# A Mamba block with a mixture of experts on one core: y's gating moves from the recurrence to GpSimd in the third stage

## Chip, cores and metric

One core of one Trainium2 chip (trn2). The metric is the device time of one execution in microseconds (us), the median of several runs. Engines are named as in the profile: PE (TensorE), DVE (VectorE), ACT (ScalarE), POOL (GpSimd), SP (SyncE, which here only issues DMAs).

## The reference

For 2048 tokens of width 512 (`x`), with `xn = layernorm(x)`, the kernel computes `x + mamba(xn) + moe(xn)`:

```python
proj = xn @ in_proj_w.T                       # 2048 x 2048
x, gate = split(proj, 2)                      # 1024 channels each
xc = silu(causal_conv(x, conv_w, 4 taps) + conv_b)
ts, B, C = split(xc @ x_proj_w.T, [32, 48])   # 16 states
dt = softplus(ts @ dt_proj_w.T + dt_proj_b)
state = state * exp(dt * A) + dt * B * xc     # one after the other over the 2048 tokens
y = sum_over_states(state * C) + xc * D
y = y * silu(gate)
mamba = y @ out_proj_w.T
```

`moe` picks 6 of 64 experts for each token (capacity 64; each expert is a SwiGLU from 512 to 352 and back) and adds a shared SwiGLU of width 704.

## The kernel before

The program has three stages. The first (`stage1`) does the layernorm, the routing, the input projection, the convolution and the gates. It stores in HBM, for each of 32 tiles, the convolved x (`xt_d`) and silu of the gate (`sz_d`), each 128 channels by 512 tokens.

The second stage, the recurrence, has 32 steps. A step i is one of 4 chunks c of 512 tokens and one of 8 blocks d of 128 channels; at the same time it does one pair of the 64 experts. Inside a step, 8 groups g of two states each run through the engines:

- PE makes dt*B*x in PSUM (`p_dBx`, L1334), with two buffers, so group g+2 starts when DVE has scanned group g.
- ACT makes exp(dt*A) (`dA`, L1173), with four buffers, so it runs four groups ahead of DVE.
- DVE scans the two states (L1023) from `dA` and `p_dBx`.
- POOL multiplies the scanned states by C (L959).
- PE sums them over the states into `p_y` (L1343), four groups at a time.

Between its groups PE does the experts' three matmuls (gate and up L1303, down L1320) and dt of the next step. Next to its scans DVE does three things. After g=1 it finishes dt of the next step (L990) and multiplies it by x (`dt_x`, L997). After g=4 it multiplies the y of the step before by silu of the gate (`gate`, L1005). After g=5 and g=6 it does the experts' products (L1040, L1044). ACT, at the end of a step, puts x*D into `p_y` (`x_times_D`, L1129), which has to wait until DVE has read the old `p_y`; PE's sum of the first four groups adds to it (`start=False`) and so waits for ACT.

What goes in which order is written out by hand: each engine runs its own list in order, and semaphores tie them. All of SP's transfers go through one queue. In step i SP issues, in this order: the next dt weights (L1462), the next gate weights of 1408 KB (L1454), C of the next chunk (L1516), 16 transfers of 64 KB that spread dt over the partitions (`spread_dt`, L851), the silu tile (L877), the store of y (L878), the up weights of 1408 KB (L1458), x of step i+2 (`load_xa`, L1450, after the sum of the first four groups, because until then `x_times_D` reads the buffer), and the down weights of 1408 KB in three transfers with rows of 2 KB (L844).

The third stage goes over the 4 chunks. For each, PE does 5.5 tiles of the shared SwiGLU (L1392) and then 14 tiles of the output sum (`out_tiles`, L1403): k = 0 to 7 are the 8 blocks of gated y, loaded as `gc` into the state's buffer; k = 8 to 13 are the shared part. Each operand is split in two parts for the matmul: ACT writes the high part (L1236, and L1216 for the shared weights), DVE subtracts it from the source to get the low part (`k_lo` L1058, `w_lo` L1052, `x_lo` L1063, `DVE out_operand_parts`, `shared_w_parts` and `x_parts` in the trace). Both parts have two buffers. POOL adds up the residuals of the chunk (L973, L977). SP loads `gc`, then the residual's inputs, then stores the four output tiles.

## Time and profile before

| | us |
|---|---|
| median of 3 runs | 1344.96 (1337.76 to 1350.12) |
| profiled execution | 1337.05 |
| its span in the trace | 1335.2 |
| busy: PE, DVE, ACT, POOL | 1233.3, 1078.3, 894.6, 866.8 |
| first stage and start of the second, about | 0 to 266 |
| recurrence, about | 266 to 1041 |
| third stage, about | 1041 to 1335 |

The span is what lies between the first and the last recorded instruction; the execution's time is 1.85 us longer. Times below are us from the start of the span. A group of instructions is named by its line, its engine and its tile; "idle before" is the time in which the engine stood still just before such an instruction, and what ended it.

### The profile page before, as it was taken

Reading aid. Unit: us, or ns where it says so; the run is one execution under the profiler, and the core shown is the slowest. Engines: PE = TensorE matmul, PEld = TensorE weight load, DVE = VectorE, ACT = ScalarE, POOL = GpSimd, SP = SyncE. Lnnn points to the kernel's source line nnn. Section 1 sums busy time; section 2 is a strip of 40 time slices with the busy share of each in tenths; the row PEclk is TensorE's granted clock in tenths of the full one; section 3 lists DMA queues with packets and bytes.
Section 4 is the critical chain, followed back from the end, with each engine's and each line's share of the span. In section 5 each row is a group of like instructions: output and inputs, shape, how many; then the busy total and the mean of one; then the engine's idle time right before and its main releaser. Section 6 shows DMA issues by size and latency. Waiting matters only on the chain.

```text
span 1335.2 us, 53004 instructions
## 1 busy us (share of the span) xinstructions
PE 1233.3 (92%) x21558; PEld 796.7 (60%) x21558; DVE 1078.3 (81%) x1235; ACT 894.6 (67%) x1925; POOL 866.8 (65%) x456
## 2 busy tenths in 40 slices
PE   6999999399999999999899998999999999999998
PEld 4777767255555555555555554455555678787876
DVE  5989888489999979899899987899999564646554
ACT  4766667287897977978878897678777243424343
POOL 3445467188989979899889997889989340303030
PEclk9999999699999989999999998999999999999999
DMA  8364554779999989999999999899898843122130
GB/s 269 122 261 160 180 207 143 244 213 283 296 302 281 319 251 274 298 282 321 281 258 316 275 309 283 260 280 290 255 325 260 282 182 139 51 102 87 63 125 31
DMA packets 131714, 305.90 MB, mean 229 GB/s; under 512 B 18400, under 2 KB 22752, under 8 KB 129824
## 3 DMA queue, kind: packets, MB, share of 16 engines
q1 hardware_dynamic: 124048, 286.18, 65.8%
q0 software_dynamic: 7600, 18.91, 7.1%
q8 instruction: 33, 0.54, 0.2%
q14 instruction: 33, 0.27, 0.1%
HBM read 214.04 MB, written 57.69 MB: 204 GB/s over the span
## 4 chain that ended last, share of the span: by engine, by line
PE 37%; ACT 11%; DMA 8%; DVE 8%; issue 8%; SPq 6%; ACTq 1%; POOL 1%; DVEq 0%; POOLq 0%
PE p_dBx L1392 7%; PE p_dBx L1334 7%; DVE state L1023 5%; SPq L851 5%; ACT dA L1173 4%; DMA xt_for_dtx<-xt_d 4%; PE p_y L1343 3%; PE p_g L1320 3%; DMA dt_blocks_odd<-step_rows 3%; PE p_y L1403 3%; PE p_g L1403 2%; PE p_u L1403 2%; PE p_dt L1403 2%; PE p_u L1303 2%; PE p_g L1303 2%
## 5 line engine op out<-in xcount | busy, mean ns | idle before, releaser
L1023 DVE TENSOR_TENSOR_SCAN state<-dA,state_carry,p_dBx 128x512 f32<-128x512 f32 x512 | 617.7, 1261 | 44.4 <-PE p_dBx L1334 42.2
L959 POOL TENSOR_TENSOR h_times_C<-state,C_bcast 128x1024 f32<-128x1024 f32 x128 | 305.0, 2388 | 62.5 <-DVE state L1023 60.9
L959 POOL TENSOR_TENSOR C_bcast<-state,C_bcast 128x1024 f32<-128x1024 f32 x128 | 315.9, 2611 | 20.4 <-DVE state L1023 19.3
L1334 PE MATMUL p_dBx<-B_diagonals,step_rows 64*32 64x128 f32 x16384 | 295.3, 275 | 29.2 <-DVE state L1023 20.1
L1334 PEld LDWEIGHTS p_dBx<-B_diagonals,step_rows 64*32 64x32 f32 x16384 | 233.2, 106 | 142.3 <-issue 140.6
L1173 ACT ACTIVATE dA<-dt_blocks_odd,A_par 128x512 f32<-128x512 f32 x256 | 169.4, 709 | 40.5 <-DMA dt_blocks_odd<-step_rows 40.5
L1173 ACT ACTIVATE dA<-dt_blocks_even,A_par 128x512 f32<-128x512 f32 x256 | 169.4, 709 | 29.5 <-DMA dt_blocks_even<-step_rows 29.5
L288 POOL TENSOR_TENSOR w_in_parts_lo<-C_bcast,w_in_parts_hi 128x512 fp32r<-128x512 f32 x64 | 96.2, 1504 | 95.2 <-ACT w_in_parts_hi L505 94.9
L973 POOL TENSOR_TENSOR step_rows<-step_rows 128x512 f32<-128x512 f32 x16 | 22.0, 1407 | 181.8 <-DMA step_rows<-moe 181.8
L384 DVE SCALAR_TENSOR_TENSOR conv_out<-conv_in,conv_w,conv_out 128x512 f32<-128x512 f32 x96 | 107.4, 1127 | 16.2 <-ACT conv_out L529 13.9
L1303 PE MATMUL p_g<-w_gate_pair,step_rows 128*64 128x352 f32 x512 | 85.0, 473 | 9.4 <-ACT step_rows L1184 9.1
L1320 PE MATMUL p_g<-w_down_pair,step_rows 128*64 128x512 f32 (+1 forms) x396 | 92.3, 601 | 0.0
L505 ACT ACTIVATE w_in_parts_hi<-C_bcast 128x512 fp32r<-128x512 f32 x64 | 40.3, 631 | 70.5 <-PE p_in L664 62.0
L1303 PE MATMUL p_u<-w_up_pair,step_rows 128*64 128x352 f32 x512 | 85.4, 475 | 2.1 <-issue 2.1
L664 PE MATMUL p_in<-xT_parts_hi,w_in_parts_lo 128*128 128x512 f32 x256 | 73.3, 408 | 8.1 <-POOL w_in_parts_lo L288 6.8
L1222 ACT ACTIVATE shared_h_rows<-p_dBx 128x512 f32<-128x512 f32 (+1 forms) x24 | 14.4, 598 | 98.2 <-PE p_dBx L1392 97.7
L1392 PE MATMUL p_dBx<-x_parts,shared_w_parts_even 128*128 128x512 f32 x288 | 69.7, 399 | 2.4 <-DVE shared_w_parts_even L1052 2.4
L1343 PE MATMUL p_y<-h_times_C,sum_over_states 128*32 128x512 f32 x512 | 62.1, 598 | 7.7 <-ACT p_y L1129 6.7
L664 PE MATMUL p_in<-xT_parts_lo,w_in_parts_hi 128*128 128x512 f32 x256 | 69.2, 392 | 0.0
L664 PE MATMUL p_in<-xT_parts_hi,w_in_parts_hi 128*128 128x512 f32 x256 | 68.5, 389 | 0.0
L945 POOL DMA_INDIRECT moe<-expert_y,scatter_lists x33 | 54.2, 1641 | 20.0 <-ACT expert_y L1145 15.0
L1074 DVE TENSOR_TENSOR shared_h_rows<-shared_h_rows,p_dBx 128x512 f32<-128x512 f32 (+1 forms) x24 | 16.5, 686 | 61.7 <-ACT shared_h_rows L1222 61.5
(185 smaller groups left out, 2062.3 us busy)
## 6 DMA issues: line engine op xcount, KB each, us to landing
w_gate_pair<-in_w_gate SPq DMA_DIRECT2D x32, 1408.0 KB
w_up_pair<-in_w_up SPq DMA_DIRECT2D x32, 1408.0 KB
w_down_pair<-in_w_down SPq DMA_DIRECT2D x66, 512.0 KB
dt_blocks_odd<-step_rows SPq DMA_DIRECT2D x256, 64.0 KB
dt_blocks_even<-step_rows SPq DMA_DIRECT2D x240, 64.0 KB
w_down_pair<-in_w_down SPq DMA_DIRECT2D x33, 384.0 KB
g_d<-y_gated SPq DMA_DIRECT2D x33, 256.0 KB, 3.8
sz_d<-silu_gate SPq DMA_DIRECT2D x32, 256.0 KB, 2.2
```

Source lines behind the costliest of these rows:

```text
L288: pool.tensor_tensor(wp[1][:, n % 2, :], win[:, tile, :], wp[0][:, n % 2, :], ALU.subtract).then_inc(s_wlo, 1)
L384: ins = dve.scalar_tensor_tensor(xt[:, d, :], xr[:, d, k:k + CH], cw[:, d, k:k + 1], xt[:, d, :], ALU.mult, ALU.add)
L664: ins = pe.matmul(pIn[n % 2][:, :], wp[p][:, n % 2, k * P:(k + 1) * P], xp[q][:, c % 2, k, :], start=at == 0, stop=at == len(parts) - 1)
L959: pool.tensor_tensor(hc[m][:, b, :, :], hb[:, q, :, :], Cb[:, NM * (c % 2) + GS * m:NM * (c % 2) + GS * m + GS, :], ALU.mult).then_inc(s_h ...
L1023: ins = dve.tensor_tensor_scan(hb[:, g % NBUF, s, :], dA[:, g % NBUF, s, :], pB[:, g % 2, :].rearrange("p (t s) -> p s t", s=GS)[:, s, :], ...
L1173: ins = act.activation(dA[:, q, s, :], dtr[u][:, b, :], ACT.Exp, scale=A[:, bass.ds(d, 1), GS * g + s:GS * g + s + 1].rearrange("p a b -> ...
L1303: ins = pe.matmul(pX[r, 0:I], xgT[:, k, r], w[:, a, k, :], start=k == 0, stop=k == KH - 1)
L1320: ins = pe.matmul(pG[r, :], hT[0:k, m, r], wd[0:k, a, m, :], start=m == 0, stop=m == len(IK) - 1)
L1334: ins = pe.matmul(out[DB * p:DB * p + DB, half, j, :, :], dtxT[k, j * P + DB * b:j * P + DB * b + DB], diag[k, ND * cp + 2 * j + p // 2, a ...
L1343: ins = pe.matmul(pY[DB * b:DB * b + DB, :], sel4[:, :], hc[m][:, b, s, :], start=False, stop=m == 1 and s == GS - 1, skip_group_check=True)
L1392: ins = pe.matmul(pX[m % 2][:, :], wparts[m % 2][:, 2 * w + a, k, :], xp[x][:, k, :], start=at == 0, stop=at == len(parts) - 1)
L1403: ins = pe.matmul(pO[j][:, :], k_parts(p, k, 0)[:, j * P:(j + 1) * P], k_parts(q, k, 1), start=k == 0 and at == 0, stop=k == NK - 1 and at ...
```

## The change

The recurrence stores y without D*x and without the gate: ACT copies `p_y` to SBUF (`take_y`, after its `dA` of g=6), PE starts the sum fresh, and DVE's `gate` and ACT's `x_times_D` are gone. In the third stage POOL gates the 8 tiles of a chunk, three instructions each (x times D, plus y, times silu), from two buffers of x and silu that SP loads tile by tile (`gate_inputs`). ACT's `k_hi` waits for the gated tile. The buffer of `gc` is loaded for the next chunk as soon as DVE has made the low parts of its 8 tiles. The down weights lie in HBM and SBUF so that both experts of a pair are one run of 4 KB. x of step i+2 is loaded ahead of the spread of dt.

```diff
-            def x_times_D(i, u, d):
-                act.wait_ge(s_xa, 16 * i + 16)
-                act.wait_ge(s_g, i + 1)
-                act.activation(pY[:, :], xa[:, u, :], ACT.Copy, scale=d).then_inc(s_xD, 1)
+            def take_y(n, u):
+                act.wait_ge(s_gst, 16 * n + 16)
+                act.wait_ge(s_sum, 2 * n + 2)
+                act.activation(gb[:, u, :], pY[:, :], ACT.Copy).then_inc(s_y, 1)
...
-            def gate(n, u):
-                dve.wait_ge(s_gst, 16 * n + 16)
-                dve.wait_ge(s_sz, 16 * n + 16)
-                dve.wait_ge(s_sum, 2 * n + 2)
-                dve.tensor_tensor(gb[:, u, :], pY[:, :], sz, ALU.mult).then_inc(s_g, 1)
...
             def load_wd(i):
                 for m, (at, k) in enumerate(IK):
-                    sp.dma_start(wd[0:k, :, m, :], io["w_down"][i][:, at:at + k, :].rearrange("a p h -> p a h")).then_inc(s_wd, 16)
+                    sp.dma_start(wd[0:k, m, :, :], io["w_down"][i][at:at + k, :, :]).then_inc(s_wd, 16)
+            def gate_inputs(c, d):
+                if ND * c + d >= 2:
+                    sp.wait_ge(s_g, ND * c + d - 1)
+                sp.dma_start(xa[:, d % 2, :], io["xt_d"][ND * c + d]).then_inc(s_gin[d % 2], 16)
+                sp.dma_start(sz[:, d % 2, :], io["sz_d"][ND * c + d]).then_inc(s_gin[d % 2], 16)
...
+                if i + 2 < STEPS:
+                    sp.wait_ge(s_dtx, i + 1)
+                    tile_in.load_xa(sp, i + 2)
                 if i + 1 < STEPS:
                     sp.wait_ge(s_dA, NG * i + 1)
                     spread_dt(i + 1)
-                sp.wait_ge(s_g, i + 1)
-                sp.dma_start(sz[:, :], io["sz_d"][i]).then_inc(s_sz, 16)
+                sp.wait_ge(s_y, i + 1)
                 sp.dma_start(io["g_d"][i], gb[:, 1 - i % 2, :]).then_inc(s_gst, 16)
...
-                sp.wait_ge(s_sum, 2 * i + 3)
-                if i + 2 < STEPS:
-                    tile_in.load_xa(sp, i + 2)
...
             sp.dma_start(gc, g_v[0]).then_inc(s_gc, 16)
+            for d in range(2):
+                gate_inputs(0, d)
...
             for c in range(1, NCH):
                 load_xT(sp, c)
+            for d in range(2, ND):
+                gate_inputs(0, d)
...
             residual_inputs(0)
-            store_out(0)
             for c in range(1, NCH):
-                sp.wait_ge(s_kused, NK * c + 2)
+                sp.wait_ge(s_klo, 2 * NK * (c - 1) + 2 * ND)
                 sp.dma_start(gc, g_v[c]).then_inc(s_gc, 16)
+                for d in range(2):
+                    gate_inputs(c, d)
+                store_out(c - 1)
+                for d in range(2, ND):
+                    gate_inputs(c, d)
                 residual_inputs(c)
-                store_out(c)
+            store_out(NCH - 1)
...
+            def gating(c, d):
+                if isinstance(d, int) and d == 0:
+                    pool.wait_ge(s_gc, 16 * c + 16)
+                pool.wait_ge(s_gin[d % 2], 16 * ND * c + 32 * (d // 2 + 1))
+                pool.tensor_tensor(xa[:, d % 2, :], xa[:, d % 2, :], Dp[:, d:d + 1].to_broadcast([P, CH]), ALU.mult).then_inc(s_xD, 1)
+                pool.wait_ge(s_xD, ND * c + (d + 1))
+                pool.tensor_tensor(gc[:, d, :], gc[:, d, :], xa[:, d % 2, :], ALU.add).then_inc(s_yD, 1)
+                pool.wait_ge(s_yD, ND * c + (d + 1))
+                pool.tensor_tensor(gc[:, d, :], gc[:, d, :], sz[:, d % 2, :], ALU.mult).then_inc(s_g, 1)
...
             scatter(STEPS)
+            for d in range(3):
+                gating(0, d)
             scatter(STEPS + 1)
+            for d in range(3, ND):
+                gating(0, d)
+            with pool.Fori(0, 1) as c:
+                residuals(c)
+            with pool.Fori(1, NCH) as c:
+                for d in range(ND):
+                    gating(c, d)
+                residuals(c)
...
             def k_hi(c, k):
                 act.wait_ge(s_kused, NK * c + (k + 1))
-                if k == 0:
-                    act.wait_ge(s_gc, 16 * c + 16)
+                if k < ND:
+                    act.wait_ge(s_g, ND * c + (k + 1))
...
                         ins = pe.matmul(pY[DB * b:DB * b + DB, :], sel4[:, :], hc[m][:, b, s, :],
-                                        start=False, stop=m == 1 and s == GS - 1, skip_group_check=True)
+                                        start=m == 0 and s == 0, stop=m == 1 and s == GS - 1, skip_group_check=True)
...
-                    pe.wait_ge(s_xD, i + 1)
+                    pe.wait_ge(s_y, i + 1)
                     sum_states(i, 0, 0)
```

SP's queue in one step of the recurrence before: `xt_for_dtx` is x of step i+2, `dt_blocks` the spread of dt.

```order
L1454 DMA w_gate_pair<-in_w_gate 128x2x1408 [waits expert_g_in_psum]
L1516 DMA C_bcast<-bc_d 32x512 [waits hc_ready]
L851 DMA dt_blocks_even<-step_rows 32x512 [waits dt_copied,dA_ready]
L851 DMA dt_blocks_even<-step_rows 32x512 x15
L877 DMA step_rows<-sz_d 128x512 [waits gated_ready]
L878 DMA g_d<-y_gated 128x512
L1458 DMA w_up_pair<-in_w_up 128x2x1408 [waits expert_u_in_psum]
L1450 DMA xt_for_dtx<-xt_d 128x512 [waits hc_summed]
L844 DMA w_down_pair<-in_w_down 128x2x512 [waits expert_y_in_psum]
```

The same stretch of SP's queue in the changed kernel:

```order
L1485 DMA w_gate_pair<-in_w_gate 128x2x1408 [waits expert_g_in_psum]
L1547 DMA C_bcast<-bc_d 32x512 [waits hc_ready]
L1481 DMA xt_for_dtx<-xt_d 128x512 [waits dtx_ready]
L852 DMA dt_blocks_odd<-step_rows 32x512 [waits dt_copied,dA_ready]
L852 DMA dt_blocks_odd<-step_rows 32x512 x15
L890 DMA g_d<-y_gated 128x512 [waits y_taken]
L1489 DMA w_up_pair<-in_w_up 128x2x1408 [waits expert_u_in_psum]
L845 DMA w_down_pair<-in_w_down 128x1024 [waits expert_y_in_psum]
```

x has moved from behind the up weights to just ahead of the spread of dt, and the silu tile is gone from the step.

SP's queue in the third stage before, from the load of one chunk's y to its stores:

```order
L927 DMA state<-g_d 128x8x512 [waits out_parts_used]
L914 DMA C_bcast<-in_x 128x4x512 [waits x_lo_ready,out_ready,residual_ready]
L915 DMA step_rows<-moe 128x4x512
L916 DMA step_rows<-moe 128x4x512
L921 DMA out<-y_gated 128x512 [waits out_ready] x4
```

The changed kernel, from the load of one chunk's y over the stores of the chunk before to the residual's inputs (two of the six later pairs of gate inputs are shown):

```order
L938 DMA state<-g_d 128x8x512 [waits out_lo_ready]
L858 DMA xt_for_dtx<-xt_d 128x512 [waits gated_ready]
L859 DMA gate_tiles<-sz_d 128x512
L858 DMA xt_for_dtx<-xt_d 128x512 [waits gated_ready]
L859 DMA gate_tiles<-sz_d 128x512
L933 DMA out<-y_gated 128x512 [waits out_ready] x4
L858 DMA xt_for_dtx<-xt_d 128x512 [waits gated_ready]
L859 DMA gate_tiles<-sz_d 128x512
L858 DMA xt_for_dtx<-xt_d 128x512 [waits gated_ready]
L859 DMA gate_tiles<-sz_d 128x512
```

Two tiles' inputs now stand ahead of the stores of the chunk before, six behind them, and the residual's inputs behind all of these.

POOL in the third stage of the changed kernel, the last tile of a chunk and what follows it:

```order
L987 TENSOR_TENSOR xt_for_dtx<-xt_for_dtx,D_par 128x512 [waits gate_inputs_loaded1]
L988 REGISTER_ALU
L989 TENSOR_TENSOR state<-state,xt_for_dtx 128x512 [waits x_times_D_ready]
L991 TENSOR_TENSOR state<-state,gate_tiles 128x512 [waits y_plus_xD_ready]
L995 ISA
L996 ISA [waits residuals_loaded]
L998 TENSOR_TENSOR step_rows<-step_rows 128x512 [waits shared_gu_in_psum]
```

In the kernel before, the first POOL instruction of a chunk is the residual's first addition; now 24 instructions stand ahead of it.

## Rows read from the trace of the kernel before

**Rows 1.** Busy time by window: PE, PEld, DVE, ACT, POOL; clock; DMA share; GB/s
```profile
266.00:1041.00 775.00, 720.94 (x19132) 397.31 (x19131) 705.05 (x677) 626.48 (x1471) 687.51 (x319) 0.99 0.94 282
1041.00:1120.50 79.50, 76.85 (x332) 58.34 (x332) 44.56 (x57) 31.14 (x53) 19.61 (x11) 0.98 0.50 179
1120.50:1190.50 70.00, 69.49 (x302) 55.97 (x301) 38.67 (x54) 27.25 (x47) 11.31 (x8) 1.00 0.26 90
900.20:922.55 22.35, 22.20 (x607) 12.33 (x602) 21.94 (x22) 18.16 (x41) 21.51 (x11) 1.00 0.91 265
```

**Rows 2.** DVE's waits, 266 to 1041: us in total, times, longest
```profile
DVE state L1023 <- PE p_dBx L1334: 42.2, 51, 3.7
DVE dt_x L997 <- DMA xt_for_dtx<-xt_d: 18.6, 16, 1.7
DVE p_dt L990 <- ACT step_rows L1115: 8.2, 11, 1.3
```

**Rows 3.** ACT's waits in the same stretch
```profile
ACT dA L1173 <- DMA dt_blocks_odd<-step_rows: 40.5, 14, 7.5
ACT dA L1173 <- DMA dt_blocks_even<-step_rows: 29.5, 12, 5.4
...
ACT p_y L1129 <- DVE y_gated L1005: 16.0, 15, 3.4
```

**Rows 4.** Groups of instructions, 266 to 1041: busy us, mean ns, idle before
```profile
L1005 DVE TENSOR_TENSOR y_gated<-p_y,step_rows 128x512 f32<-128x512 f32 x32 | 21.3, 667 | 0.0
...
L1129 ACT ACTIVATE p_y<-xt_for_dtx,D_par 128x512 f32<-128x512 f32 x32 | 21.8, 682 | 16.0 <-DVE y_gated L1005 16.0
```

**Rows 5.** Timeline of one step: start, duration, engine; x's issue and its use
```profile
697.85 0.52 SPq L1450 DMA_DIRECT2D xt_for_dtx<-xt_d  x1
...
706.35 0.69 DVE L997 TENSOR_TENSOR dt_x<-p_dt,xt_for_dtx 128x512 f32<-128x512 f32 x1 [1.43 <-DMA xt_for_dtx<-xt_d]
```

**Rows 6.** SP's timeline in another step: the spread of dt
```profile
883.26 10.12 SPq L851 DMA_DIRECT2D dt_blocks_even<-step_rows  x16
```

**Rows 7.** DVE's timeline in the third stage, before and while POOL adds residuals
```profile
1138.56 0.69 DVE L1052 TENSOR_TENSOR shared_w_parts_even<-w_gate_pair,shared_w_parts_even 128x512 fp32r<-128x512 f32 x1
...
1143.57 0.69 DVE L1074 TENSOR_TENSOR shared_h_rows<-shared_h_rows,p_dBx 128x512 f32<-128x512 f32 x1 [3.72 <-ACT shared_h_rows L1222]
...
1147.01 1.79 DVE L1058 TENSOR_TENSOR out_operand_parts<-state,out_operand_parts 128x512 fp32r<-128x512 f32 x1
```

**Rows 8.** POOL's timeline in the third stage: residual additions, chunk 0 (first half) and 1
```profile
1085.79 6.72 POOL L973 TENSOR_TENSOR step_rows<-step_rows 128x512 f32<-128x512 f32 x4 [23.38 <-DMA step_rows<-moe]
...
1140.33 5.04 POOL L973 TENSOR_TENSOR step_rows<-step_rows 128x512 f32<-128x512 f32 x4 [41.02 <-DMA step_rows<-moe]
1145.33 6.32 POOL L977 TENSOR_TENSOR C_bcast<-C_bcast,step_rows 128x512 f32 x4
```

**Rows 9.** PE's timeline, chunk 0: first matmuls of output tiles k = 2, 3, 6, 7
```profile
1084.70 0.84 PE L1403 MATMUL p_y<-out_operand_parts 128*128 128x512 f32 x3
...
1088.11 0.93 PE L1403 MATMUL p_y<-out_operand_parts 128*128 128x512 f32 x3 [0.52 <-DVE out_operand_parts L1058]
...
1098.30 0.93 PE L1403 MATMUL p_y<-out_operand_parts 128*128 128x512 f32 x3 [0.43 <-DVE out_operand_parts L1058]
...
1101.11 0.84 PE L1403 MATMUL p_y<-out_operand_parts 128*128 128x512 f32 x3
```

**Rows 10.** SP's timeline at the start of the third stage
```profile
1043.84 0.37 SPq L895 DMA_DIRECT2D state<-g_d  x1
...
1059.87 2.81 SPq L900 DMA_DIRECT2D w_down_pair<-in_sw_down  x6
```

**Rows 11.** DMA issues: count, KB each, median us from issue to landing
```profile
state<-g_d SPq DMA_DIRECT2D x4, 2048.0 KB, 8.6
step_rows<-moe SPq DMA_DIRECT2D x8, 1024.0 KB, 14.1
...
h_times_C<-in_w_out SPq DMA_DIRECT2D x1, 2048.0 KB, 10.5
```

47 lines of the change are left out of this document (24 added, 23 removed).

## The prediction

> **What bounds the kernel now.** I read the busy table by window first, then the waits of the engine that is busiest in the long window, then the timelines where the change puts work. The window from 266 to 1041 is the recurrence: in its 775 us DVE is busy 705.05 and PE 720.94 [rows 1]. The reader is to see that two engines are nearly full at once. DVE's waits there are 42.2 us on PE's `p_dBx`, 18.6 on the load of x and 8.2 on ACT's part of dt [rows 2]; with 705.05 that makes 774, so DVE's list accounts for the whole stretch, 24.2 us a step over 32 steps. One step, from 900.20 to 922.55, shows the pace when nothing is late: 22.35 us, with PE busy for 22.20 of it [rows 1]. PE's own work is therefore about 22.35 a step, and 32 x 22.35 = 715 us is the least that the recurrence can take while its matmuls stay as they are. At most 60 us can be won there.
>
> In the third stage the picture is another one. From 1120.5 to 1190.5, one chunk, PE is busy 69.49 of 70.00 us, DVE 38.67, ACT 27.25 and POOL 11.31 [rows 1]. PE bounds it without gaps, so nothing can be won there, and what is added to POOL costs time only where it makes PE wait.
>
> **The change part by part: the recurrence.** DVE loses 32 gates of 667 ns, 21.3 us; ACT swaps one copy of 682 ns for another of the same shape, at no cost, and loses the 16.0 us for which the old one waited for the gate [rows 3, 4]. The gate stands after the scan of g=4, just where PE has the up matmuls between its groups; in the step of 22.35 us the gate was in DVE's list and PE still hardly idled [rows 1]. There the 667 ns are hidden and their removal gives nothing: DVE will wait for `p_dBx` instead. In steps where DVE is late for another reason they count. The bounds are 0 and 21.3; I take a third, 7 us, because the unhurried step is the nearest row.
>
> The wait for x, 18.6 us in 16 steps [rows 2], goes: x was issued at 697.85, behind 1408 KB of up weights, and DVE used it at 706.35 after a wait of 1.43 [rows 5]. It now has a whole step. What is late next is the spread of dt. Its 16 issues take SP 10.12 us [rows 6], and ACT already waits 40.5 + 29.5 = 70 us for its blocks [rows 3]. x's 256 KB now stand directly ahead of it; at the 282 GB/s of the stretch [rows 1] that is 0.9 us more, against the same amount saved by the silu tile that no longer comes. ACT runs four groups ahead of DVE, so most of its lateness never reaches DVE; what did is the 8.2 us. I count 14 of the 18.6 us, and 3 of the 8.2 because dt is made earlier. The bounds are 6 (the spread takes over most of the wait) and 27 (all of both).
>
> Together the recurrence wins 7 + 14 + 3 = 24 us, between 6 and 46; the upper end leaves 729 us, or 22.8 a step, as close to PE's pace as I allow, since a new chunk and the first steps also cost.
>
> The down weights in runs of 4 KB: I cost this at 0. No row has one transfer in both forms; the nearest are two loads of 2048 KB, y in 2 KB runs in 8.6 us and the output weights in 16 KB runs in 10.5 with other loads ahead [rows 11], which show no gain of long runs. The bounds are -5 and +2. The Trainium skill, "DMA: Bandwidth & Descriptors", section "Specifications", asks for 512 B or more for line rate, which both forms have; by it the term is 0, too, and no run here shows 4 KB.
>
> **The change part by part: the third stage.** POOL gets 32 tiles of three dependent instructions, 96 in all. Alone, a sum of two 128x512 tiles takes POOL 5.04 / 4 = 1.26 us, beside a busy DVE 6.32 / 4 = 1.58 to 6.72 / 4 = 1.68 [rows 8]. With about 0.15 us for each wait between them (an estimate) a tile is 4.2 us alone and 5.2 when DVE is busy. The Trainium skill, "GPSIMD Engine Reference", section 3.1, gives about 2.6 cycles for an element of a two-input operation at 1.2 GHz; as an estimate from that page 512 elements are 1.11 us and a tile 3.8, which would end chunk 0's gating 3 us sooner and make this term 33 instead of the 36 below.
>
> The price is on DVE. While POOL adds, a DVE subtraction with both inputs in SBUF takes 1.79 us instead of 0.69; the product with an input in PSUM stays at 0.69 [rows 7]. An output tile then costs PE (1098.30 - 1088.11) / 3 = 3.40 us instead of 2.72 to 2.81 [rows 9], so each 3.4 us of POOL work beside the output tiles cost 0.68.
>
> Chunk 0: y's load is issued at 1043.84 [rows 10], and with the weights ahead of it the first tile can start at about 1060. Tiles 0 and 1 follow, but the inputs of tile 2 stand behind the shared down weights and three loads of xn, 4.5 MB in all, issued from 1059.87 on [rows 10], so they land at about 1076. Tiles 2 to 7 and the scatter between them then take 6 x 4.9 + 1.6 = 31 us, to 1107. Tile k = 7 started at 1101.11 [rows 9] and now starts at about 1107.5: +6. The residual's inputs are issued only when tile 5 is gated (about 1097) and take 14.1 us [rows 11], so POOL's additions, 13.5 us, lie beside k = 8 to 12, where DVE also does `x_lo` of the next chunk: two tiles with 3 contended subtractions (5.3 us instead of 2.7) and two with 2, 2 x 2.6 + 2 x 0.7 = 6.6. Chunk 0 costs +13.
>
> Chunks 1 to 3: tiles 0 and 1 are gated beside the last output tiles of the chunk before (9 us of POOL, +1.7, for chunks 1 and 2 booked there). Tiles 2 to 7 start about 6 us after the chunk, behind four stores, and end at about +34. From +23 (the product at 1143.57 in a chunk that began at 1120.5 [rows 7]) to +38 DVE has 12 subtractions for the last shared and the first output operands; contended, they take 12 x 1.79 = 21 us instead of 8, and k = 1 and 2 wait about 2. The residual's inputs are issued at about +24, when tile 5 is gated, and land at about +36 with nothing ahead of them, so its additions now lie beside output tiles k = 2 to 6 and cost another 4. That is 8 for each of chunks 1 and 2, and 7 for chunk 3 without a following one.
>
> The third stage loses 13 + 8 + 8 + 7 = 36 us. The bounds are 10 (POOL's phases fall between DVE's; chunk 0 alone pays) and 60 (every one of the 96 instructions delays one DVE subtraction by 1.1 us, 106 us, of which the idle half of DVE hides less than half).
>
> **The sum.** -24 + 36 = +12. Against the profiled execution, 1337.05, that is 1349; the median of the runs shown is 7.9 higher, which would make it 1357. I say 1353, between the two. Of a difference of 1%, 13 us, a measurement of this kernel can about tell that it is one; my sum lies just at that edge.
>
> **The rivals.**
> 1. The recurrence falls to PE's pace: with neither gate nor late x, DVE is ahead of PE in nearly every step, and the mean step goes from 24.2 to 22.8 us, -46, while the third stage costs half of my sum, 20. For it speaks the step of 22.35 us; against it, that 42.2 us of DVE's waits are on PE already. It decides if the mean step is under 23.0 us. Time: 1345 - 26 = 1319, faster.
> 2. The spread of dt takes x's place: its wait on ACT grows, dt comes late, and the recurrence wins only 6; the third stage costs 36. For it speak the 70 us of ACT's waits and the place of x in the queue. Time: 1345 + 30 = 1375, slower.
> 3. POOL's work is mostly hidden: the contended subtractions fall into DVE's idle half, the third stage costs only what chunk 0's late tiles and the residual's new place cost, 20, and the recurrence wins 24. Time: 1345 - 4 = 1341, no change.
>
> **How the numbers follow.** My forecast has 0.40, of which 0.29 is slower by over 1% and 0.11 within. Rival 1 has 0.20 (faster 0.19, same 0.01). Rival 2 has 0.16, all slower. Rival 3 has 0.24: faster 0.04, same 0.19, slower 0.01. So faster 0.23, same 0.31, slower 0.46. The range from 1320 to 1381 reaches from rival 1 to somewhat past rival 2; the likeliest case's own range is 1340 to 1366.
>
> **What would show it.** Right: no wait of `dt_x` on `xt_for_dtx`; DVE's waits on `p_dBx` larger than 42.2 us; a mean step near 23.4; in the third stage `out_operand_parts` and `shared_w_parts` on DVE often at 1.3 to 1.8 us; ACT waiting for POOL's gated tile at k = 3 to 7 of chunk 0; residual additions beside the output tiles; chunks of 77 to 78 us instead of 70. Wrong: chunks still of 70 to 72 us, or a recurrence under 735 us.

## The result, and the profile after

The changed kernel takes 1370.1 us (median of 4 runs, 1361.2 to 1379.9), the kernel before in runs beside it 1347.5 (1337.8 to 1355.8): the ratio is 1.0185 with a 95% interval of 1.0139 to 1.0231, slower by some 23 us. The profiled executions stand at 1365.71 (span 1363.9) and 1337.05 (span 1335.2); that of before is the fastest of its runs, so differences against it come out some 6 us too large, and the place for that is the recurrence: in every profile taken of a kernel with the old third stage, that stage took 292 to 294 us.

Busy time of the changed kernel by window (the recurrence, then the four chunks of the third stage), with the columns of [rows 1]:

```profile
266.00:1031.00 765.00, 744.27 (x19118) 404.45 (x19120) 680.34 (x641) 624.16 (x1470) 683.93 (x318) 1.00 0.93 275
1038.80:1133.50 94.70, 82.67 (x332) 61.12 (x332) 59.45 (x55) 28.88 (x50) 59.73 (x40) 0.93 0.62 215
1133.50:1209.00 75.50, 70.77 (x302) 55.59 (x301) 52.72 (x54) 27.36 (x47) 47.08 (x32) 1.00 0.42 139
1209.00:1285.10 76.10, 71.11 (x301) 55.51 (x301) 56.00 (x54) 27.35 (x47) 47.74 (x32) 1.00 0.40 138
1285.10:1359.20 74.10, 70.62 (x301) 55.67 (x300) 49.28 (x50) 25.54 (x46) 38.70 (x26) 1.00 0.29 101
```

The same windows of the third stage in the kernel before, as far as [rows 1] lacks them:

```profile
1041.80:1120.50 78.70, 76.85 (x332) 58.34 (x332) 43.76 (x56) 30.34 (x52) 18.95 (x11) 0.98 0.50 179
1190.50:1260.30 69.80, 69.48 (x301) 55.97 (x300) 38.50 (x54) 27.25 (x47) 11.33 (x8) 1.00 0.25 90
1260.30:1330.50 70.20, 69.59 (x301) 55.99 (x300) 36.36 (x50) 25.57 (x46) 11.79 (x8) 1.00 0.26 91
```

The chunks are 16.0, 5.5, 6.3 and 3.9 us longer: the third stage loses 31.7. The recurrence, which should have given 24 back, gave 3: its first step begins 0.4 us later than before, and the third stage starts at 1038.8 instead of 1041.8. (From the first to the last step it is 6 us shorter, 745.0 instead of 750.8; PE then stands 4.7 us for the first shared weights instead of 2.4.) Where the gain went is read from the waits (us in total, times, longest) from 266 to 1041. The changed kernel's:

```profile
DVE state L1055 <- PE p_dBx L1365: 81.9, 116, 4.8
...
PE p_g L1334 <- ACT step_rows L1213: 2.9, 5, 1.1
PE p_dBx L1365 <- DVE state L1055: 1.6, 4, 0.5
```

PE's in the kernel before:

```profile
PE p_dBx L1334 <- DVE state L1023: 20.1, 16, 2.2
PE p_g L1303 <- ACT step_rows L1184: 9.1, 10, 1.2
...
PE p_y L1343 <- ACT p_y L1129: 6.7, 15, 0.6
PE p_dt L1283 <- ACT step_rows L1137: 4.6, 3, 3.2
```

DVE's waits for x, 18.6 us [rows 2], are gone, and so are the gates, 21.3 us [rows 4]; nearly all of it, 39.7 us, reappears as waiting for PE, 81.9 instead of 42.2. PE's own waits fell from 20.1 + 9.1 + 6.7 + 4.6 = 40.5 us to 4.5. So PE should have been done 36 us sooner. It was not, because its own matmuls took longer. The two groups that grew (busy us, mean ns of one, idle before), before:

```profile
L1334 PE MATMUL p_dBx<-B_diagonals,step_rows 64*32 64x128 f32 x16320 | 293.3, 275 | 28.6 <-DVE state L1023 20.1 <-issue 8.4
L1343 PE MATMUL p_y<-C_bcast,sum_over_states 128*32 128x512 f32 x512 | 62.0, 598 | 0.0
```

and after:

```profile
L1365 PE MATMUL p_dBx<-B_diagonals,step_rows 64*32 64x128 f32 x16320 | 303.5, 274 | 15.9 <-issue 13.4 <-DVE state L1055 1.6
L1374 PE MATMUL p_y<-C_bcast,sum_over_states 128*32 128x512 f32 x512 | 84.8, 600 | 0.8
```

The same 512 sums over the second half of the states fill 84.8 us instead of 62.0, the same dBx matmuls 303.5 instead of 293.3: 33 us more, with an unchanged duration of the single matmul. Sixteen sums of 0.6 us each take 1.92 us, so they run side by side; the time grows when they start one behind the other. The start flag that the change adds is not it: it stands on the other half of the sums, which took 62.1 in both. That was the question for the experiments: what makes PE slower as soon as it no longer waits?

### The profile page after: what moved, and what is told of

Same layout as the page of the kernel before. It is cut to its first block, busy times and chain, and to the rows that moved or that the text cites. A ratio compares the mean times of both kernels' runs of the same rounds, so it can differ in the third digit from the quotient of the medians.

```text
span 1363.9 us, 53050 instructions
## 1 busy us (share of the span) xinstructions
PE 1268.5 (93%) x21558; PEld 805.1 (59%) x21558; DVE 1120.4 (82%) x1202; ACT 893.4 (66%) x1926; POOL 1009.8 (74%) x551
## 4 chain that ended last, share of the span: by engine, by line
PE 59%; DVE 7%; issue 5%; ACT 3%; DMA 3%; POOL 3%; SPq 1%; ACTq 0%; DVEq 0%; POOLq 0%
PE p_dBx L1365 18%; PE p_y L1374 9%; PE p_dBx L1423 6%; PE p_g L1351 6%; PE p_g L1334 5%; PE p_u L1334 5%; DVE out_operand_parts L1088 4%; PE p_y L1434 2%; PE p_u L1434 1%; PE p_g L1434 1%; PE p_dt L1434 1%; PE p_u L1320 1%; DVE state L1055 1%; DMA dt_blocks_odd<-step_rows 1%; PE p_dt L1327 1%
## 5 line engine op out<-in xcount | busy, mean ns | idle before, releaser
L1055 DVE TENSOR_TENSOR_SCAN state<-dA,state_carry,p_dBx 128x512 f32<-128x512 f32 x512 | 619.7, 1262 | 82.0 <-PE p_dBx L1365 81.9
L975 POOL TENSOR_TENSOR C_bcast<-state,C_bcast 128x1024 f32<-128x1024 f32 x128 | 319.7, 2731 | 8.3 <-DVE state L1055 7.9
L1365 PE MATMUL p_dBx<-B_diagonals,step_rows 64*32 64x128 f32 x16384 | 305.5, 274 | 16.6 <-issue 13.4
L1365 PEld LDWEIGHTS p_dBx<-B_diagonals,step_rows 64*32 64x32 f32 x16384 | 236.4, 105 | 137.0 <-issue 134.1
L987 POOL TENSOR_TENSOR xt_for_dtx<-xt_for_dtx,D_par 128x512 f32<-128x512 f32 x32 | 42.1, 1316 | 79.8 <-DMA gate_tiles<-sz_d 79.7
L1374 PE MATMUL p_y<-C_bcast,sum_over_states 128*32 128x512 f32 x528 | 86.7, 600 | 0.8
L1434 PE MATMUL p_y<-out_operand_parts 128*128 128x512 f32 (+1 forms) x168 | 51.5, 415 | 25.2 <-DVE out_operand_parts L1088 24.9
L664 PE MATMUL p_in<-xT_parts_lo,w_in_parts_hi 128*128 128x512 f32 x256 | 68.9, 391 | 0.0
L1423 PEld LDWEIGHTS p_dBx<-x_parts,shared_w_parts_even 128*128 128x128 f32 x288 | 54.7, 192 | 19.1 <-issue 7.4
```

The source lines that it names most:

```text
L664: ins = pe.matmul(pIn[n % 2][:, :], wp[p][:, n % 2, k * P:(k + 1) * P], xp[q][:, c % 2, k, :], start=at == 0, stop=at == len(parts) - 1)
L975: pool.tensor_tensor(hc[m][:, b, :, :], hb[:, q, :, :], Cb[:, NM * (c % 2) + GS * m:NM * (c % 2) + GS * m + GS, :], ALU.mult).then_inc(s_h ...
L1055: ins = dve.tensor_tensor_scan(hb[:, g % NBUF, s, :], dA[:, g % NBUF, s, :], pB[:, g % 2, :].rearrange("p (t s) -> p s t", s=GS)[:, s, :], ...
L1365: ins = pe.matmul(out[DB * p:DB * p + DB, half, j, :, :], dtxT[k, j * P + DB * b:j * P + DB * b + DB], diag[k, ND * cp + 2 * j + p // 2, a ...
L1374: ins = pe.matmul(pY[DB * b:DB * b + DB, :], sel4[:, :], hc[m][:, b, s, :], start=m == 0 and s == 0, stop=m == 1 and s == GS - 1, skip_gro ...
L1423: ins = pe.matmul(pX[m % 2][:, :], wparts[m % 2][:, 2 * w + a, k, :], xp[x][:, k, :], start=at == 0, stop=at == len(parts) - 1)
```

## The experiments

In the tables below the recurrence is measured in each profile from the first to the last step's down matmuls, the third stage from the first shared tile to the end; the ratio is to the kernel before, run beside each.

```
kernel                     recurrence  third stage  median us  ratio [95%]
before                        750.8       293.4       (1348-1352)
changed                       745.0       325.1       1370.1   1.0185 [1.0139, 1.0231]
e1  sum moved                 749.0       328.6       1375.2   1.0188 [1.0153, 1.0223]
e2  dt projection twice       768.2       324.8       1386.4   1.0272 [1.0241, 1.0303]
e3  no gating                 752.4       312.9       1359.1   1.0066 [1.0041, 1.0091]
e4  x early alone             770.3       292.3       1352.3   1.0025 [0.9993, 1.0057]
e5  indirect DMAs moved       720.4       323.6       1344.0   0.9971 [0.9944, 0.9998]
e6  before, DMAs moved        784.1       293.2       1373.2   1.0159 [1.0113, 1.0204]
e7  x early, DMAs moved       770.4       293.8       1362.3   1.0097 [1.0065, 1.0129]
e8  tiles 2, 3 first          746.7       321.6       1366.8   1.0141 [1.0100, 1.0183]
e9  one product               735.3       301.8       1333.5   0.9864 [0.9826, 0.9901]
e10 no indirect DMAs          701.5       324.6       1319.3   0.9763 [0.9731, 0.9795]
e11 residuals first           751.8       294.5       1344.1   0.9950 [0.9920, 0.9980]
e12 4 KB weights alone        763.1       292.3       1344.9   0.9987 [0.9961, 1.0013]
```

### e1 and e2: is PE short of instructions?

```diff
-                    dBx(i, cp, 2)
                     sum_states(i, 1, 1)
+                    dBx(i, cp, 2)
```

> The changed kernel, with PE's sum over the second half of the states (16 matmuls) moved from behind the third dBx group of a step to ahead of it, right behind the gate matmuls. In the changed kernel this sum takes 2.5 to 3.0 us in 25 of 32 steps where it took 1.92 before, and a step takes 23.8 us though PE waits for nothing. Theory A (a TensorE that never waits is short of instructions: it uses up its lead in the dBx groups, 128 instructions in 1.09 us each, and the sum behind them then gets its instructions late and loses the step between its four column groups): behind the slow gate matmuls the lead is there, the sum takes 1.92 us again, a step 22.6 to 23.0 us, and the recurrence is 25 to 35 us shorter than in the changed kernel: some 1338 us. Theory B (the sum is slow because of what it reads or of the flag that starts its accumulation, wherever it stands): it stays at 2.5 to 3.0 us, a step at 23.8 us and the time within 5 us of the changed kernel's.

Measured: all 33 sums at 1.92 us, and yet nothing gained. PE waits for DVE's scans again, which it had stopped doing; the third dBx group now stands 1.9 us later, and DVE gets its input late. The row of PE's waits, 266 to 1041:

```profile
PE p_dBx L1365 <- DVE state L1055: 37.1, 31, 1.2
```

Both theories missed. What stays: in e1, as in the kernel before, PE waits over a microsecond a step (37.1 us in 31 waits) and has fast sums.

```diff
                 pe.wait_ge(s_wdt, 32 * n + 32)
+                pe.matmul(pM[:, :], wdt[:, :], ts[:, :], start=True, stop=True)
                 pe.matmul(pM[:, :], wdt[:, :], ts[:, :], start=True, stop=True).then_inc(s_dtps, 1)
```

> The changed kernel, with the dt projection of each step (one 512-column matmul of 0.49 us) made twice, to the same result: PE gets more work, in which few instructions pass. Theory A (short of instructions): the half microsecond lets the instructions catch up, the sum over the second half of the states falls from 3.0 to 1.92 us in most steps, and a step is not longer than 23.8 us, rather 23.1 to 23.4: the whole 10 to 20 us faster than the changed kernel although PE does more. Theory B (the sum is slow for another reason): the sum stays at 2.5 to 3.0 us, a step is 0.4 us longer, the whole 10 to 15 us slower than the changed kernel.

Measured: slower by another 16 us, and the sums at 1.92 us. Theory A had the sums right, but falls: time to catch up gives nothing back. Theory B had the time about right, but falls too, for the stall left the sum and went into the dBx group ahead of it. One step of e2 beside one of the changed kernel shows where it stays. First e2 (start, duration; PE and GpSimd's gather):

```profile
617.93 1.06 PE L1366 MATMUL p_dBx<-B_diagonals,step_rows 64*32 64x128 f32 x51
618.55 1.01 POOL L953 DMA_INDIRECT tokens_of_pair<-xn_d,gather_lists  x1
619.19 0.28 PE L1366 MATMUL p_dBx<-B_diagonals,step_rows 64*32 64x128 f32 x1 [0.19 <-issue]
619.93 0.50 PE L1366 MATMUL p_dBx<-B_diagonals,step_rows 64*32 64x128 f32 x12 [0.46 <-issue]
```

Then the changed kernel, with the weight load (PEld) at which the sum's stall ends, and its other stall, in the last dBx group beside the scatter:

```profile
622.90 1.60 POOL L961 DMA_INDIRECT moe<-expert_y,scatter_lists  x1 [0.15 <-issue]
623.30 0.84 PE L1365 MATMUL p_dBx<-B_diagonals,step_rows 64*32 64x128 f32 x35
624.30 0.72 PE L1365 MATMUL p_dBx<-B_diagonals,step_rows 64*32 64x128 f32 x29 [0.16 <-issue]
...
634.14 1.01 POOL L953 DMA_INDIRECT tokens_of_pair<-xn_d,gather_lists  x1
634.38 3.03 PE L1374 MATMUL p_y<-C_bcast,sum_over_states 128*32 128x512 f32 x16
...
635.50 0.17 PEld L1374 LDWEIGHTS p_y<-C_bcast,sum_over_states 128*32 128x32 f32 x7 [0.63 <-issue]
```

In e2 PE stalls behind its 51st dBx matmul, in the changed kernel within the sum: other instructions. But the stall ends 619.93 - 618.55 = 1.38 us after the gather's start in the one and 635.50 - 634.14 = 1.36 in the other. It is so in the whole recurrence: at 28 of the 31 gathers of the changed kernel from 286 us on, and at all 31 of e2, an idle time of 0.4 to 0.8 us of the weight loads, put down to "issue", ends 1.27 to 1.38 us after the gather's start. It keeps time with GpSimd, not with PE's program, and "issue" says that PE waited for nothing that the profile shows. The stall shown is over 1.36 us after the start, while the gathers of this kernel land 8.8 us after theirs (median). The Trainium skill, "Perfetto Trace Analysis", section "DMA Instruction — SWDGE (GPSIMD)", says that such a row lasts until the descriptors are written, not until the data are there. The trace agrees, with a row of 1.01 us; by that, the stall shown, from 634.87 to 635.50, lies in the time in which GpSimd's cores write descriptors (until 635.15) and just behind it.

The gather of the kernel before stands at the same place, and its sums don't suffer (start and duration):

```profile
343.85 1.01 POOL L937 DMA_INDIRECT tokens_of_pair<-xn_d,gather_lists  x1 [0.16 <-issue]
344.08 1.92 PE L1343 MATMUL p_y<-C_bcast,sum_over_states 128*32 128x512 f32 x16
```

That gave theory C: PE gets no new instructions while GpSimd starts an indirect DMA (the instruction that fetches or adds rows by a list of indices, here the gather and the scatter), and a PE that has waited in this step or the last has some in store.

### e5 and e10: move the indirect DMAs, leave them out

```diff
-GATHER_AT, SCATTER_AT = 0, 4
+GATHER_AT, SCATTER_AT = 0, 5
...
+                    if g == GATHER_AT:
+                        pool.wait_ge(s_xT, i + 1)
+                        gather(i + 1)
                     pool.wait_ge(s_sum, 2 * i + (m + 1))
...
-                    if g == GATHER_AT:
-                        pool.wait_ge(s_xT, i + 1)
-                        gather(i + 1)
```

> The changed kernel, with GpSimd's two indirect DMAs of a step moved: the gather ahead of the step's first product with C instead of behind it, so that it falls beside PE's gate matmuls (32 instructions in 2.5 us), the scatter one product later, beside the down matmuls. The extra dt projection did not bring the time of the sum back: PE's stalls only moved in its program, and stayed where they were against GpSimd: 0.7 us from 0.6 us after a gather's start, 0.6 us from 0.9 us after a scatter's. Theory C (while GpSimd starts an indirect DMA TensorE gets no new instructions, and loses what it has not in store; the kernel before had them in store because PE waited over a microsecond a step): the sum over the second half of the states takes 1.92 us in nearly all steps, the last dBx group 1.09 us instead of 1.77, a step 22.5 to 23.3 us instead of 23.8, the recurrence 15 to 35 us shorter than in the changed kernel: 1335 to 1355 us. Rival D (the stalls belong to PE's own program and only keep step with GpSimd): they stay in the sum and in the last dBx group, a step at 23.6 to 24 us and the time within 6 us of the changed kernel's.

Measured: 26 us faster than the changed kernel, the recurrence 24.6 shorter. The groups of e5, 266 to 1007:

```profile
L1365 PE MATMUL p_dBx<-B_diagonals,step_rows 64*32 64x128 f32 x16320 | 299.2, 275 | 8.7 <-issue 7.6 <-DVE state L1055 0.3
L1374 PE MATMUL p_y<-C_bcast,sum_over_states 128*32 128x512 f32 x512 | 62.0, 598 | 0.0
```

The sums are back at 62.0 us; half of the steps take 22.5 us or less. The dBx groups keep part of their excess: the gather now starts shortly before the gate matmuls end, and the dBx group behind them still loses time (in the step with a gather at 640.08 the group at 640.66 takes 1.43 us instead of 1.16). For e10, GpSimd's gathers and scatters were replaced by their semaphore updates (no tokens are fetched, no expert rows added).

```diff
-                pool.indirect_dma_start(xg[:, :], None, io["xn_d"],
-                                        bass.IndirectOffsetOnAxis(ap=gidx[:, n:n + 1].bitcast(U32), axis=0)).then_inc(s_xg, 16)
+                pool.sem_inc(s_xg2, 16)
...
-                pool.indirect_dma_start(io["moe"], bass.IndirectOffsetOnAxis(ap=rows_of_pair.bitcast(U32), axis=0),
-                                        yo[:, n % 2, :], None, compute_op=ALU.add).then_inc(s_sc, 16)
+                pool.sem_inc(s_sc2, 16)
```

> The changed kernel without GpSimd's indirect DMAs in the recurrence and behind it (no tokens are gathered and no expert rows scattered; the waits and the order of everything else stay). Theory C (PE's stalls are what an indirect DMA's start takes from a TensorE that has no instructions in store): the sums take 1.92 us in nearly all steps, the last dBx group 1.09 us, a step 22.4 to 23.2 us, the recurrence 20 to 40 us shorter than in the changed kernel. Rival D (what the move changed was the order of GpSimd's products, not the stalls' cause): the stalls stay where they were in PE's program, a step at 23.5 us or more.

Measured: 1319.3 us, the recurrence 43.5 us shorter than in the changed kernel. The groups of e10, 266 to 989:

```profile
L1365 PE MATMUL p_dBx<-B_diagonals,step_rows 64*32 64x128 f32 x16320 | 290.1, 274 | 8.8 <-issue 8.3 <-DVE state L1055 0.2
L1374 PE MATMUL p_y<-C_bcast,sum_over_states 128*32 128x512 f32 x512 | 62.4, 598 | 0.0
```

The dBx group is under that of the kernel before and the sums are within 0.4 us of it, so the 33 us are the indirect DMAs'. The rest of e10's gain probably has a second cause: with the rows themselves left out the queues are lighter (DMA share 0.85 instead of 0.93), and ACT waits 14 us for dt instead of 58. That PE's instructions are what stands still is argued from "issue" and from the part that PE's waits play; no view shows it. Nor do e5 and e10 tell the start of an indirect DMA from the transfers that it sets off, since they move or remove both together; for the start speaks only the constant distance above.

### e4 and e12: one part of the change alone

```diff
+                if i + 2 < STEPS:
+                    sp.wait_ge(s_dtx, i + 1)
+                    tile_in.load_xa(sp, i + 2)
...
-                sp.wait_ge(s_sum, 2 * i + 3)
-                if i + 2 < STEPS:
-                    tile_in.load_xa(sp, i + 2)
...
-        self.xa = sb("xt_for_dtx", [P, 2, CH])
+        self.xa = sb("xt_for_dtx", [P, 4, CH])
```

> The kernel before with x alone loaded a step ahead, as the change does it, into four buffers instead of two (the gate stays in the recurrence on DVE, D times x on ACT, the third stage as before). The forecast priced this part at 14 us in the recurrence. Theory A (TensorE is the bound behind it, and one that doesn't wait gets its instructions late): the wait of DVE for x goes (18.6 us before), DVE waits for dBx instead, over 55 us against 42.2, the sum over the second half of the states goes over 2.3 us in part of the steps, and the recurrence gains 2 to 8 us: within 1% of the kernel before. Rival (x was a wait of its own): it gains 12 to 18 us, and the sums stay at 1.92 us.

> The kernel before with the down weights alone in runs of 4 KB instead of 2 KB. The forecast priced this part at nothing (bounds 5 us faster to 2 us slower), since no wait in the trace names the down weights. Right: within 5 us of the kernel before, with some 15,000 fewer DMA packets. Wrong: a gain of 10 us or more, which would mean that the packets themselves hold up the dt blocks and x, on which ACT and DVE wait.

(The edit of e12 is the change's own, in the layout and the load of the down weights.) Neither moved the time, as expected: 1.0025 and 0.9987. But both did what they were to do. Waits of e4, 266 to 1041, then of e12:

```profile
DVE state L1024 <- PE p_dBx L1337: 79.0, 94, 4.2
```

```profile
DVE state L1023 <- PE p_dBx L1334: 69.8, 87, 4.6
DVE dt_x L997 <- DMA xt_for_dtx<-xt_d: 5.7, 6, 2.4
...
ACT dA L1173 <- DMA dt_blocks_odd<-step_rows: 20.3, 10, 5.3
...
ACT dA L1173 <- DMA dt_blocks_even<-step_rows: 11.8, 10, 4.2
```

In e4 DVE's wait for x is gone; in e12 it falls from 18.6 to 5.7 and ACT's wait for dt from 70 to 32 us, with 79,649 DMA packets in that stretch instead of 91,194 (11,500 fewer, not the 15,000 that were expected). In both DVE waits for PE instead, and the sums are slow (79.3 us for 496, 86.6 for 512). Each part alone runs into the same stall; it is not a matter of the gate.

The second half of theory C, that earlier waits of PE hide the stall, is not settled by these runs. In the kernel before a sum is fast 10 us behind a wait of 2.16 us; in e12 one is slow 12 us behind a wait of 2.15 at the same place of the step. First the kernel before, then e12 (start, duration):

```profile
893.31 1.15 PE L1334 MATMUL p_dBx<-B_diagonals,step_rows 64*32 64x128 f32 x64 [2.16 <-DVE state L1023]
...
903.81 1.92 PE L1343 MATMUL p_y<-C_bcast,sum_over_states 128*32 128x512 f32 x16
```

```profile
997.77 1.15 PE L1334 MATMUL p_dBx<-B_diagonals,step_rows 64*32 64x128 f32 x64 [2.15 <-DVE state L1023]
...
1009.96 3.01 PE L1343 MATMUL p_y<-C_bcast,sum_over_states 128*32 128x512 f32 x16
```

In the kernel before 1 of 32 sums takes over 2.2 us, in e4 and e12, where PE waits less, 21 and 27 do: that much stands. When a wait protects a sum, and how, is open.

### e6 and e7: the move without the change

The same two moves in the kernel before, and in e4:

> The kernel before with the same two moves of GpSimd's indirect DMAs. Theory C: there PE waits in each step and has instructions in store when the DMAs start (its sums take 1.92 us already), so nothing is to be had: within 1% of the kernel before, 1340 to 1355 us. Against C would speak a gain over 1%: then the indirect DMAs cost the kernel before something that its sums do not show.

> The kernel before with x loaded a step ahead (four buffers) and the two indirect DMAs moved; the gate stays in the recurrence, so the third stage keeps its 293 us. Theory C: now the 18.6 us of DVE's wait for x come out at the end, since PE no longer loses its stalls: 10 to 25 us faster than the kernel before, 1323 to 1339 us, the sums at 1.92 us. Rival (PE and DVE hold each other through the two dBx buffers, whatever the sums take): within 1% of the kernel before.

Both missed: 1.6% and 1.0% slower. Their sums are fast (62.3 us in e6), so the stall is not what they lose to. In e6 it is x:

```profile
DVE dt_x L997 <- DMA xt_for_dtx<-xt_d: 43.2, 19, 5.2
```

There x's load waits for y's sum, and that for GpSimd's products, which now stand behind the gather. In e7 GpSimd itself waits for ACT before it may gather, and everything behind the gather on GpSimd waits with it:

```profile
POOL tokens_of_pair L937 <- ACT step_rows L1187: 32.0, 11, 8.2
```

Why ACT is late there is left open. The moved gather waits for ACT in e5 and e6 too, 14.9 us in each, so this wait alone does not tell where the move pays; in e5, where it paid, there were slow sums to win back and no load of x behind GpSimd's products.

### e3, e8 and e11: the third stage

In e3 the three operations of a tile are left out; in e11 also the residual's loads and additions of chunks 1 to 3 go ahead of tiles 2 to 7; e8 is the whole change with two tiles' loads moved.

```diff
-                pool.tensor_tensor(xa[:, d % 2, :], xa[:, d % 2, :], Dp[:, d:d + 1].to_broadcast([P, CH]), ALU.mult).then_inc(s_xD, 1)
...
-                pool.tensor_tensor(gc[:, d, :], gc[:, d, :], sz[:, d % 2, :], ALU.mult).then_inc(s_g, 1)
+                pool.sem_inc(s_g, 1)
```

> The changed kernel without the 96 GpSimd instructions of the gating in the third stage (D times x, the sum and the product with silu of the gate are left out; the loads and the order stay). Theory 1 (the third stage lost its 32 us to these instructions: DVE's subtractions slowed beside them, and tile 2 of the first chunk late): the third stage is back at 290 to 296 us, chunks 1 to 3 at 70 to 71 us each, and the whole some 30 us faster than the changed kernel. Theory 2 (a good part comes from the loads and from y being read back later in SP's order): the third stage stays over 305 us.

> The changed kernel without the gating's GpSimd operations (left out, as before), and with the residual's loads and additions of chunks 1 to 3 ahead of the loads of gating tiles 2 to 7 instead of behind them. Without the gating those chunks still took 74.5 us, with the additions beside PE's first output tiles, where they ran beside the shared expert's matmuls in the kernel before. If that is what the 4.5 us a chunk are: the additions start some 7 us earlier, and chunks 1 and 2 take 70 to 71.5 us. If it is the loads themselves or PE's clock: they stay at 73.5 us or more. The first chunk is not touched (83 to 85 us).

Windows of e3, chunks 0 and 1, then of e11:

```profile
1051.90:1135.50 83.60, 78.11 (x331) 59.48 (x331) 42.28 (x55) 28.77 (x50) 15.82 (x10) 0.96 0.70 243
1135.50:1210.00 74.50, 71.09 (x301) 57.18 (x300) 40.15 (x54) 27.24 (x47) 12.70 (x8) 0.98 0.41 142
```

```profile
1051.20:1134.10 82.90, 78.03 (x332) 59.39 (x332) 41.70 (x55) 28.78 (x50) 16.18 (x10) 0.96 0.72 245
1134.10:1203.00 68.90, 68.90 (x301) 56.11 (x300) 36.85 (x54) 27.25 (x47) 11.15 (x8) 1.00 0.44 153
```

Theory 2 holds: without the gating's 96 instructions the third stage wins only 12 of the 32 us, 11 of them in chunk 0. In chunks 1 and 2, with the gating left out, the rest of the loss is the residual: its additions started 27 us into the chunk in e3 (1237.30 in the one that began at 1210.0), into PE's output tiles at 31; in e11 at 14.5 (1217.52), beside the shared matmuls, as in the kernel before [rows 8], and PE has no gap at all (68.9 us a chunk, less than the 70 to 71.5 expected). From e3 to e11 the third stage gets 18.4 us shorter, by that order alone; what the order would give with the gating in place was not tried.

```diff
+            for d in range(2, 4):
+                gate_inputs(0, d)
             for c in range(1, NCH):
                 load_xT(sp, c)
-            for d in range(2, ND):
+            for d in range(4, ND):
                 gate_inputs(0, d)
```

> The changed kernel with the gating inputs of tiles 2 and 3 of the first chunk issued ahead of the 3 MB of x for the shared expert instead of behind them. In the changed kernel GpSimd waits 11.2 us for tile 2, which lands at 1073.7 us, and PE stands still 4.3 us for its third output tile, after which its clock is at half for two tiles. If the late tile 2 makes the first chunk long: tile 2 lands some 6 us earlier, the gating of tile 7 ends some 6 to 10 us earlier, PE's 4.3 us go, and the first chunk takes 84 to 90 us instead of 94.6: 5 to 10 us faster than the changed kernel. If the pace of GpSimd's tiles (4.9 us each) does, and not where they begin: the first chunk stays over 92 us.

Measured: tile 2 comes 27.4 us into the chunk instead of 34.9, and the chunk takes 92.6 us, 2 less: the pace, not the beginning. PE still stands 3.53 us ahead of output tile k = 2, though that tile is gated by 1071.8 and its matmuls start at 1087.93. What the pace costs is seen in the changed kernel's chunk 0. One of DVE's subtractions, PE's matmuls and the start of GpSimd's residual additions (start, duration, idle before):

```profile
1083.49 1.75 DVE L1088 TENSOR_TENSOR out_operand_parts<-state,out_operand_parts 128x512 fp32r<-128x512 f32 x1
1086.83 1.62 PE L1434 MATMUL p_y<-out_operand_parts 128*128 128x512 f32 x3 [4.28 <-DVE out_operand_parts L1088]
1088.25 1.48 PE L1434 MATMUL p_g<-out_operand_parts 128*128 128x512 f32 x3
...
1093.91 0.85 PE L1434 MATMUL p_u<-out_operand_parts 128*128 128x512 f32 x3
...
1107.66 6.06 POOL L998 TENSOR_TENSOR step_rows<-step_rows 128x512 f32<-128x512 f32 x4 [4.28 <-DMA step_rows<-moe]
...
1117.79 0.93 PE L1434 MATMUL p_y<-out_operand_parts 128*128 128x512 f32 x3 [2.06 <-DVE out_operand_parts L1088]
```

The clock behind PE's first stop, and behind those at the residual's additions, in windows of their own:

```profile
1086.80:1092.10 5.30, 5.27 (x13) 4.14 (x14) 3.25 (x2) 0.00 (x0) 5.14 (x4) 0.50 0.39 133
1123.60:1126.90 3.30, 3.30 (x9) 2.55 (x8) 2.26 (x2) 0.00 (x0) 3.14 (x4) 0.52 0.00 0
```

PE stands for 4.28 us ahead of tile k = 2. That tile's gating had ended at 1078.3; what came late are DVE's low parts, for from 1080.16 on four of its subtractions in a row take 1.52 to 1.77 us beside GpSimd instead of 0.69. Then PE's granted clock is 0.50 (1.2 of 2.4 GHz) for 5.3 us, and three matmuls take 1.48 us instead of 0.85. Beside the residual's additions it stands three times for 1.46 to 2.06 us, and the clock is at 0.52 for another 3.3 us. In all PE is idle 12.0 us of this chunk instead of 1.9, and busy 82.67 instead of 76.85, some 4.3 of these 5.8 us at half clock (an estimate from the distance of the groups' starts, up to 1.28 instead of 0.69 us): 16 us.

### e9: a version that beats both

e5's order, with D times x put back on ACT in the recurrence, and a single product for GpSimd in the third stage:

```diff
+                act.activation(pY[:, :], xa[:, v, :], ACT.Copy, scale=d).then_inc(s_xD, 1)
...
+                pool.tensor_tensor(gc[:, d, :], gc[:, d, :], xa[:, d % 4, :], ALU.mult).then_inc(s_g, 1)
```

> The changed kernel with the moved indirect DMAs, and with D times x put back into the recurrence as the kernel before has it: ACT writes it into p_y behind its copy of y, and PE's sums start on top of it (x is loaded into four buffers, a step ahead still). The third stage is left with one GpSimd product a tile instead of three operations, and with half of the loads, four tiles ahead instead of two. If the third stage's 32 us come from GpSimd's work and from what it pushes back, it falls to 300 to 312 us from 325 while the recurrence keeps the step of 22.5 us that the moved DMAs gave: 1318 to 1335 us, faster than the kernel before. Rival: ACT's 0.57 us a step and PE's wait for it take the recurrence's gain back (a step over 23.2 us): 1340 to 1355 us.

Measured: 1333.5 us, 0.9864 of the kernel before and 37 us under the changed one. The third stage falls to 301.8 us as expected; the recurrence keeps the step (22.5 us in the median) and pays in a few long steps, 735 us against e5's 720; what makes these long was not traced. Chunk 0:

```profile
1029.10:1113.20 84.10, 78.75 (x332) 58.63 (x332) 49.16 (x55) 28.90 (x50) 35.47 (x22) 0.97 0.62 219
```

## Why the prediction was right, and where not

The direction and the range held: slower, at 1370 within 1320 to 1381, beyond the likeliest case's own 1340 to 1366. The measured difference, some 23 us, is twice the sum of +12. With the recurrence as forecast the outcome would have been 1347.5 - 24 + 31.7 = 1355, slower by 0.6%: the sign comes from the third stage, as was said, but that the loss is clear of 1% is luck, for it comes from the step that failed. And 1370 lies in the range by its upper end, which was drawn for rival 2. The two terms fared differently.

- **The recurrence, -24: this step failed.** It measured -3 by the start of the third stage in the two profiles, -6 from step to step, and by medians some -9 (22.6 slower in all, less 31.7). The mean step was 24.0 us, not 23.4. The waits moved as said: x's wait gone, DVE's waits for `p_dBx` far over 42.2, ACT's waits for dt down to 58 us from 70. The mistake was PE's floor, "PE's own work is therefore about 22.35 a step", taken from one step that began at 900.20. PE had stood 2.16 us for DVE 7 us before it, until 893.31. In the changed kernel, where PE hardly waits, the median step takes 23.8, because its two indirect DMAs cost PE over a microsecond in it (without them, in e10, 22.1); the average step of before, 24.2, was nearly at that already. With those starts moved (e5) the recurrence gains 30 us on before, within the bounds of 6 to 46.
- **The gate, 7, and x, 14:** x alone gave nothing (e4); it was hidden behind PE. The gate alone was not tried; in the changed kernel its 21.3 us came back as waits for PE.
- **The down weights, 0:** right in the time (e12), wrong in the reason. The shorter list of packets took 13 us off DVE's wait for x and 38 off ACT's waits, and PE's stalls took that back.
- **The third stage, +36:** 31.7. Chunk 0 cost 16 instead of 13, chunks 1 to 3 5.5, 6.3 and 3.9 instead of 8, 8 and 7. Tile 2's inputs landed at 1073.7 (said: 1076), the gating of chunk 0 ended at 1103.4 (1107), tile k = 7 began at 1105.6 (1107.5), in a stage that itself began 3 us earlier than the one from which those times were counted; the residual's additions ran beside output tiles. The mechanism, DVE's subtractions slowed beside GpSimd, held. (For chunk 3 the parts named there add up to 6, not 7.) Too much was put down to the gating's own contention in the later chunks, where e3 and e11 give most of it to the residual's new place; too little to the same contention in chunk 0, for PE's stop at k = 2 and the half clock behind it stood in no step. ACT waited for a gated tile only twice (8.1 us), not at each of k = 3 to 7.
- **GpSimd's price:** a tile took 3.8 us alone (1058.68 to 1062.45) and 4.9 beside DVE, less than the 4.2 and 5.2 that were said. Beside DVE most operations took 1.49 to 1.64 us. The Trainium skill, "GPSIMD Engine Reference", section 3.1, has 2.6 cycles for an element, from which 1.11 us for an operation and 3.8 for a tile had been estimated. The trace agrees for the sum of the tile alone, not for its parts (1.04, 1.29 and 1.29 us, with 0.08 between them); there the measurement decides.
- **The rivals:** the outcome has the sizes of rival 2 (1375), but not its cause: ACT's waits for the spread of dt became shorter, 58 us instead of 70.

## What to carry to other kernels

The pace of an engine is not read from the one step in which nothing was late: look at what it did just before, and whether it ever runs that fast for several steps together. When a wait is removed and the next engine becomes the bound, ask what its own waits had been hiding, and compare the busy time of the same instructions in both traces: 62.0 against 84.8 us told more here than any wait. And work that is moved to an idle engine pushes back what that engine already did; when the new work was left out 12 of the third stage's 32 us went, and when the old work was then put back in its earlier place another 18.

## What the runs showed of the hardware

- With the gather's row on GpSimd (1.0 us) or the scatter's (1.6 us) TensorE loses time: a dBx group takes 1.7 us (623.30 to 625.02) to 2.5 us (617.93 to 620.43 in e2) instead of 1.16, and 16 sums that run side by side take 3.0 instead of 1.92 us. With these DMAs moved the recurrence is 24.6 us shorter (e5), without them 43 (e10). In the kernel before, the same gathers cost the sums nothing; what protects them there is argued, not shown.
- TensorE's busy share in the recurrence was 97% (744.27 of 765), its weight loads' 53% (404.45). The Trainium skill, "Perfetto Trace Analysis", section "Identifying the Most-Contended Engine", would judge its headroom by the weight loads and by the share of the peak that the matmuls reach. Here the trace differs, for TensorE was the bound: DVE waited 81.9 us for it. But the busy share is no pure measure either, since the 84.8 us of the sums contain their stalls.
- A VectorE subtraction with both inputs in SBUF took 1.52 to 1.77 us while GpSimd gated (1080.16 to 1086.69), 0.69 while it did not.
- A pause of TensorE of 4.28 us was followed by 5.3 us at a granted clock of 0.50 (1.2 of 2.4 GHz), and three pauses of 1.46, 2.06 and 1.87 us, one about every 5 us, by 3.3 us at 0.52.
